# A 128x128 counter tile written by GpSimd between every two gathers of a graph kernel's edge passes

## The reference

```
h  = relu(layernorm(x))
x1 = prelu(GAT(h))                      # 4 heads: softmax over the edges of a destination, weighted sum of h[src]
x  = x + prelu(attention(x1) + x1 @ Wskip)   # q[dst] . k[src], softmax, weighted sum of v[src]
h  = relu(layernorm(x))
x  = x + layernorm(h2 + gelu(h2 @ W1) @ W2)  # h2 = layernorm(GAT(h, 8 heads, 2 edge types) + h)
```

## Time and profile before

| | us |
|---|---|
| time, median of 3 runs | 3976.72 (3972.66 to 3978.0) |
| span of the profiled execution, which is the only time of that execution on record | 4992.2 |
| "gat" pass in the trace, first gather to end of the last | 1336.4 |
| "attn" pass, the same | 1289.1 |
| "typed" pass, the same | 1348.0 |
| all that lies before, between and behind these three stretches | 1018.7 |

### The profile page before, as it was taken

How to read it: one execution, slowest core, us unless ns; L and a number is a source line. 1 busy time by engine, 2 the same in 40 slices (tenths; PEclk the granted TensorE clock), 3 DMA queues, 4 the chain that set the end, 5 groups by cost and what they waited for, 6 DMA issues and landing times. The chain is left out here.

```text
span 4992.2 us, 80536 instructions
## 1 busy us (share of the span) xinstructions
PE 3385.8 (68%) x15489; PEld 2315.7 (46%) x15489; DVE 3110.9 (62%) x10883; ACT 1739.5 (35%) x5661; POOL 2633.7 (53%) x2962
## 2 busy tenths in 40 slices
PE   6366665666677467777777778556666666666999
PEld 4244443444445344444444445334444444433998
DVE  6355555655567555666666667656666666667886
ACT  3333333333335444545455555311121221121332
POOL 3555555555540345555555543555555555553787
PEclk8666677776769788888888889767777777677999
DMA  4444444444433433333333334534433333332221
GB/s 144 134 127 122 125 121 122 127 123 126 122 97 90 129 94 105 107 106 107 103 108 108 110 86 150 182 106 112 112 108 110 111 108 108 109 107 81 72 73 53
DMA packets 286529, 554.64 MB, mean 111 GB/s; under 512 B 83599, under 2 KB 180941, under 8 KB 286126
## 3 DMA queue, kind: packets, MB, share of 16 engines
q0 software_dynamic: 115872, 326.30, 23.8%
q10 hardware_dynamic: 97688, 160.93, 10.6%
q1 hardware_dynamic: 72566, 63.01, 4.5%
HBM read 473.68 MB, written 76.32 MB: 110 GB/s over the span
## 5 line engine op out<-in xcount | busy, mean ns | idle before, releaser
L483 PE MATMUL psum<-big,onehots_or_distances 128*128 128x264 f32 (+2 forms) x4992 | 2151.6, 541 | 1058.1 <-DVE acc L654 486.6
L483 PEld LDWEIGHTS psum<-big,onehots_or_distances 128*128 128x128 f32 x4992 | 1025.5, 250 | 1419.8 <-issue 1274.7
L654 DVE TENSOR_TENSOR acc<-acc,psum 128x264 f32 (+2 forms) x2496 | 1046.1, 419 | 773.7 <-DMA acc<-in_edges_dram,acc 237.2
L267 POOL DMA_INDIRECT big<-table_attn,src_by_edge x782 | 739.8, 946 | 764.5 <-SPq L260 352.2
L267 POOL DMA_INDIRECT big<-table_typed,src_by_edge x782 | 740.3, 947 | 618.7 <-SPq L260 380.8
L267 POOL DMA_INDIRECT big<-table_gat,src_by_edge x782 | 739.2, 945 | 608.5 <-SPq L260 379.1
L373 ACT ACTIVATE onehots_or_distances<-psum 128x512 f32<-128x512 f32 x416 | 248.1, 596 | 1665.6 <-DMA joins<-visit_joins 524.3
L632 DVE TENSOR_TENSOR big<-big,psum 128x256 f32<-128x256 f32 x1664 | 669.1, 407 | 91.6 <-issue 58.7
L426 PE MATMUL psum<-big,onehot_t 128*128 x2496 | 490.5, 311 | 228.7 <-issue 138.8
L508 DVE SCALAR_TENSOR_TENSOR dot_products<-psum,big 128x258 f32<-128x258 f32 x832 | 348.1, 419 | 449.0 <-PE psum L426 228.0
L344 ACT ACTIVATE onehots_or_distances<-iota,tables 128x128 f32<-128x128 f32 x832 | 330.3, 397 | 669.1 <-DVE acc L654 428.5
(11 more groups left out here) (280 smaller groups left out, 4192.3 us busy)
## 6 DMA issues: line engine op xcount, KB each, us to landing
onehot_t<-onehots ACTq DMA_DIRECT2D x68, 512.0 KB
big<-visit_positions ACTq DMA_DIRECT2D x52, 512.0 KB
onehots<-big ACTq DMA_DIRECT2D x36, 512.0 KB
big<-onehots ACTq DMA_DIRECT2D x36, 512.0 KB
big<-in_x_dram SPq DMA_DIRECT2D x98, 128.0 KB, 2.8
big<-table_gat,src_by_edge POOLq DMA_INDIRECT x782
big<-table_attn,src_by_edge POOLq DMA_INDIRECT x782
big<-table_typed,src_by_edge POOLq DMA_INDIRECT x782
```

The costliest lines, as they stand in the source:

```text
L267: pool.indirect_dma_start(X[:, t % RING, :], None, ph.table, bass.IndirectOffsetOnAxis(ap=m.src[:, t:t + 1], axis=0)).then_inc(S[f"rows{t ...
L483: nc.tensor.matmul(sum_ps(v), onehot_at(v), rows, start=True, stop=True).then_inc(S["summed"], 1)
L654: nc.vector.tensor_tensor(row, row, sum_ps(v), ALU.add).then_inc(S["added"], 1)
```

## The change

Between each two gathers of a pass GpSimd writes a tile of 128x128 numbers (each row counts from 0 to 127) into a new buffer `pause` that nobody reads. Each write raises a new semaphore "paused", and the gather with number t waits until t such writes are done. The write itself waits for no semaphore.

```
@@ edge_pass, block.gpsimd @@
             for t in range(NT):
                 if t >= RING and t % QUARTER == 0:
                     pool.wait_ge(S["freed"], t // QUARTER - groups + 1)
+                if t:
+                    pool.wait_ge(S["paused"], t)
                 pool.indirect_dma_start(X[:, t % RING, :], None, ph.table,
                                         bass.IndirectOffsetOnAxis(ap=m.src[:, t:t + 1], axis=0)).then_inc(S[f"rows{t // QUARTER % groups}"], 16)
+                nc.gpsimd.iota(m.pause[:, :], [[1, P]], base=0, channel_multiplier=0, allow_small_or_imprecise_dtypes=True).then_inc(S["paused"], 1)
@@ build_program @@
+        m.pause = sb("pause", [P, P])
```

## The result

The changed kernel takes 4795.37 us (4792.51 to 4797.14, 3 runs) against 3976.72: 1.2064 times as long, with a 95% interval of 1.2042 to 1.2085, or 819 us more. The forecast was 4420 us, the range ended at 4640.

The account below looks back on a forecast made before the run. GpSimd's gathers were taken to bound the passes: 3 x 782 x 1.46 = 3425 us, plus 1018.7 of all else, plus 0 to 25 of stops, minus up to 60 of tails: 4384 to 4469, forecast 4420 us, range 4150 to 4640.

Parts of the forecast that it names:

- GpSimd sets the pace in timed runs: Edge passes: GpSimd gathers without stops, 782 x 1.25 = 977.5 us a pass, against 986 in timed runs.
- The rival in which the idle time of rows 2 and 5 covers the cost: Passes: GpSimd's added 493 us fall into 1041 us of waiting, time stays at 3977; chance 0.08.
- The rule on the profile's total: Whole kernel: a 6.2 us gap would keep the trace's stops in timed passes; rejected, the gap here being 1015.5 us.
- The write: GpSimd between gathers: a 128x128 write takes 0.24 us and starts 0.01 us after the gather.
- The wait of an ordinary gather: Between write and next gather: 0.08 us of wait plus 0.18 us of start, giving 1.46 us from gather to gather.
- the price of the next gather: Each of 782 gathers a pass: 0.13 to 0.33 us more than the 1.25 us spacing, middle 0.21.
- The prediction's own sign of being wrong: Timed runs rising by more than 3 x 782 times the added spacing would mean the consumers lose as well.
- GpSimd need of 3425: Three passes on GpSimd: 3 x 782 x 1.46 = 3425 us.
- the rest it had as 995: Beside GpSimd's need: 1018.7 us outside the passes, plus 0 to 25 of stops, minus up to 60 of shorter tails.
- The cover: GpSimd's stops in the passes, 25.5 us in all, up to 27 absorbed; tails allowed 20 us each, 60 in all.
- The profiled span of 5000 to 5250: Changed kernel's profile: much of the 493 us falls into GpSimd's 1041 us of idle, so a smaller rise.
- Going by spacing: GpSimd's added cost in the passes: 782 x 3 x 0.21 = 493 us by spacing, against 554 by write spans.

Follow-up runs that it names:

- second profile: The kernel before, unedited, timed and profiled once more: 3976.44 us, profile span 3974.8 us.
- the run with the wait that doesn't bite: Changed kernel with two tiles written by turns, each gather waiting for the write before the last: 4250.27 us.
- the run with the lone wait everywhere: Changed kernel; gathers with one wait also wait for "cleared", written ahead of the wait for the write: 5759.24 us.
- the run with a second wait only: Kernel before, no write; the first gather of each group of 4 also waits for a second semaphore, meant to be long met: 3973.08 us.

## Why the prediction was wrong

**GpSimd sets the pace in timed runs: right.** The prediction put the timed passes at 986 us each against a need of 977.5, and rejected the cover that its own trace showed. The second profile has passes of 992, 1002 and 981 us, with gathers in a run 1.25 us apart. The rival in which the idle time of rows 2 and 5 covers the cost has fallen. What made TensorE and VectorE stand still for 8 us in the long execution was not tried and stays open.

**The rule on the profile's total.** The page "Runtime: NRT & Kernel Launch" of the Trainium skill, section "The ~15µs preamble/postamble breakdown", has a profile's total about 6.2 us above the execution time, whatever the kernel. No run here shows that figure: the profiled execution of the changed kernel took 4792.51 us with a span, from the first instruction to the last, of 4790.9, which is 1.6 us less. But the two lie microseconds apart, and so do those of the second profile of the kernel before, 3976.83 and 3974.8. So the 1015 us of the first profile were that execution's own, as the prediction's reading needed.

**The write: right.** 0.24 us was taken; it lasts 0.25, and starts 0.01 us behind the gather.

**The wait of an ordinary gather: right.** 0.08 + 0.18 = 0.26 us were taken, 0.27 measured (0.11 and 0.16 by the run with the wait that doesn't bite); spacing 1.49 us where 1.46 was forecast. Over 596 x 3 gathers the 0.03 us make 54 us.

**The step that failed: the price of the next gather, taken the same for all 782.** The prediction bounded it between 0.13 and 0.33 us and applied that to each gather. At 185 group starts of a pass the gather has two waits, and the rows of the order in the section on the change showed it. There the added time is 2.00 - 1.25 = 0.75 us, over twice the upper bound. The prediction said nothing of a second wait on one gather and so put it at nothing, without a reason. The ring place is indeed free by then; but one of the two waits is an instruction of its own, it was the one for the write, and what stands behind it in the queue starts 0.5 us later than a gather that holds that wait itself. This term is 185 x 3 x (2.00 - 1.46) = 300 us. No row of before held a gather with two waits, so nothing bounded its price from above. The prediction's own sign of being wrong came true as well: the rise of 819 is above 3 x 782 times the added spacing of 0.24, 563. But the reason that it gave, that the consumers lose too, did not: SyncE never waited for them.

**The sum again, with the measured prices.** 596 x 1.493 + 185 x 2.00 = 1260 us a pass. Three of them make 3780, all else 970.5, and 10 or 11 short stops a pass, together about 31 us: 4781, against a span of 4790.9. The forecast's GpSimd need of 3425 was short by 355, and the rest it had as 995 in its 4420 was 25 too long.

**The cover: about right in sum.** The kernel before had 42 us of stops in its passes, and the time outside the passes shrank by 30; the forecast allowed 25 and 60.

**The profiled span of 5000 to 5250: wrong.** It carried the stops of the long execution over into a kernel that does not have them.

**Going by spacing.** The page "Perfetto Trace Analysis" of the Trainium skill, section "GPSIMD Engine Instruction", advises to time GpSimd by the spacing of starts and not by the spans. The trace agrees: the spans of the writes, 2346 x 0.253 = 593 us, are 253 short of the 846 us by which the passes grew, mostly because the longer gap in front of a group start, 0.78 us at 555 of them, is in no instruction's span.

## What to carry to other kernels

Before an idle share in a profile is counted as cover, compare the profiled span with the timed runs: where they differ, take the idle time out of the span and see whether the rest is the timed run. GpSimd, with gathers back to back, was full at 75% busy (741 of the 992 us of "gat" in the second profile), since the gap in front of each gather belongs to its need.

When an instruction gets a second wait, look which of the two will stand alone in the queue, and write the waits so that it is the one that is met early. In every run here it was the one written last, right ahead of the gather. The order of two lines was worth 272 us.

## What the runs showed of the hardware

- On GpSimd's queue an indirect DMA that holds its wait itself starts 0.27 us after the write that it waits for; behind a lone wait met by the same write, 0.78 us after (changed kernel, and nearly all gathers of the run with the lone wait everywhere). A lone wait that is met one gather earlier costs nothing (1.49 us in the run with the order changed; 3973 us in the run with a second wait only). No gather of these runs starts less than 0.74 us behind its lone wait, and at four group starts of the run with the order changed, where it passed 1.1 to 1.2 us ahead, the spacing stayed at 1.49. This fits a queue that makes the next DMA ready while the engine works, and that a wait standing alone holds up; the queue's lead is seen in the run with a second wait only, what it does in the 0.74 us is not.
- Passes with writes have nine further stops in front of a gather that no semaphore explains, where the kernel before had none in "typed". The idle time there is 1.4 us in most runs, 0.4 us in the run where the write's wait does not bite and 2.7 us with a lone wait everywhere:

```profile
1002.63 0.96 POOL L269 DMA_INDIRECT big<-table_gat,src_by_edge  x1 [1.39 <-issue]
```

  This row is of the run with the order changed. In every pass of each of the seven kernels with writes the nine stand before the same gathers, the 114th and then every 76th. Loads of instructions, after so many instructions each, don't explain that: between two stops GpSimd's queue has 171 instructions in the changed kernel, 114 in the run with writes at group starts alone and 228 with a lone wait everywhere. The cause stays open.
- A write of 128x1 counters lasted 0.12 us in the first stage (at 1.17 us) and 0.15 us in the passes, both in the run with the small write.
